# Taking the rest of a projection on VectorE, straight from the PSUM bank

## The reference

```python
x = x + LN(attention(LN(x)))
x = x + LN(experts(LN(x)))
```

```python
qkv = x @ W_in.T + b_in
scores = einsum("bhqd,bhkd->bhqk", q, k) * scale + mask
a = softmax(scores); o = a @ v; return o @ W_out.T + b_out
...
fused = w[0] * local_out + w[1] * global_out   # w = softmax(fusion_w)
```

## Time and profile before

| what | value |
|---|---|
| median of 3 runs | 1818.97 us (1818.25 to 1822.79) |
| the profiled execution | 1818.58 us, its span 1816.8 us |
| busy: PE, DVE | 1636.8 us, 1226.7 us |
| busy: ACT, POOL | 993.6 us, 884.3 us |

### The profile page before, as it was taken

How to read it: one execution, slowest core, us unless ns; L and a number is a source line. 1 busy time by engine, 2 the same in 40 slices (tenths; PEclk the granted TensorE clock), 3 DMA queues, 4 the chain that set the end, 5 groups by cost and what they waited for, 6 DMA issues and landing times.

```text
span 1816.8 us, 43072 instructions
## 1 busy us (share of the span) xinstructions
PE 1636.8 (90%) x14472; PEld 1184.8 (65%) x14472; DVE 1226.7 (68%) x3673; ACT 993.6 (55%) x2251; POOL 884.3 (49%) x1173
## 2 busy tenths in 40 slices
PE   5779999999999999999999999999999846999993
PEld 3457777777776676766676776777776634666662
DVE  2446777777777776777777777777777534777773
ACT  2356666666666666666666666666666531111210
POOL 3224545445445555545554444444444341666665
PEclk9789999999999999999999999999999967999997
DMA  6985555555555555555555555555555202444540
GB/s 138 222 181 98 95 96 97 96 95 96 97 94 96 96 96 94 95 94 94 93 92 91 91 93 94 94 92 94 92 84 97 67 13 74 146 138 140 153 126 10
DMA packets 254346, 183.59 MB, mean 101 GB/s; under 512 B 30116, under 2 KB 252775, under 8 KB 254142
## 3 DMA queue, kind: packets, MB, share of 16 engines
q1 hardware_dynamic: 245150, 176.22, 48.9%
q0 software_dynamic: 7168, 3.73, 1.2%
q10 hardware_dynamic: 1824, 1.06, 0.2%
HBM read 55.78 MB, written 38.04 MB: 52 GB/s over the span
## 4 chain that ended last, share of the span: by engine, by line
PE 59%; POOL 17%; issue 8%; DVE 6%; SPq 4%; ACT 3%; DVEq 2%; DMA 1%; POOLq 0%; ACTq 0%
PE bank L1147 11%; PE bank L1275 7%; PE bank L1184 5%; PE bank L1178 4%; PE bank L1129 4%; PE bank L1116 4%; PE bank L1137 3%; POOL out L632 3%; POOL zb L627 3%; PE bank L1175 3%; PE bank L1108 3%; PE bank L1104 3%; PE bank L1154 3%; SPq L422 2%; POOL ybuf L583 2%
## 5 line engine op out<-in xcount | busy, mean ns | idle before, releaser
L883 DVE TENSOR_REDUCE mx<-bank 128x2 f32<-128x512 f32 (+1 forms) x768 | 513.3, 685 | 134.1 <-PE bank L1175 87.2
L674 ACT ACTIVATE pt<-bank 128x512 f32<-128x512 f32 x768 | 448.2, 601 | 160.2 <-PE bank L1116 130.2
L550 POOL TENSOR_TENSOR rest<-x,parts 128x512 f32<-128x512 f32 x128 | 148.5, 1160 | 295.7 <-ACT x L688 295.7
L1147 PE MATMUL bank<-xnT,weff 128*128 128x256 f32 x1024 | 247.4, 385 | 2.4 <-ACT x L688 1.7
L1178 PE MATMUL bank<-stack 96*128 96x256 bf16 x1024 | 198.9, 276 | 20.6 <-DVE mx L883 19.6
L688 ACT ACTIVATE parts<-bank,bqk 128x256 bf16<-128x256 f32 x256 | 107.5, 471 | 173.4 <-PE bank L1147 160.4
L1147 PEld LDWEIGHTS bank<-xnT,weff 128*128 128x128 f32 x1024 | 185.9, 191 | 23.8 <-ACT x L688 2.1
L555 POOL TENSOR_TENSOR parts<-rest,parts 128x512 bf16<-128x512 f32 x128 | 148.4, 1160 | 107.7 <-DVE parts L871 107.7
L1116 PE MATMUL bank<-stack 100*128 100x128 bf16 x2048 | 198.9, 219 | 0.0
L1116 PEld LDWEIGHTS bank<-stack 100*128 100x128 bf16 x2048 | 158.9, 98 | 12.5
L1178 PEld LDWEIGHTS bank<-stack 96*128 96x128 bf16 x1024 | 79.5, 98 | 125.2 <-issue 57.4
(11 more groups left out here) (149 smaller groups left out, 3144.3 us busy)
## 6 DMA issues: line engine op xcount, KB each, us to landing
stack<-parts SPq DMA_DIRECT2D x384, 128.0 KB, 6.7
stack<-parts SPq DMA_DIRECT2D x768, 64.0 KB, 2.6
slots_scratch<-zeros SPq DMA_DIRECT2D x5, 2080.0 KB, 11.9
erows<-slots_scratch SPq DMA_DIRECT2D x64, 130.0 KB
xr<-x SPq DMA_DIRECT2D x32, 256.0 KB, 7.2
out<-obuf SPq DMA_DIRECT2D x32, 256.0 KB, 2.1
ew<-w_gate SPq DMA_DIRECT2D x32, 256.0 KB, 3.2
ew<-w_up SPq DMA_DIRECT2D x32, 256.0 KB, 3.5
```

The costliest lines, as they stand in the source:

```text
L550: pool.tensor_tensor(rest[:, j % 2, :], x32[:, j % 2, :], parts[:, j, 0, :], ALU.subtract).then_inc(rest_ready, 1)
L674: act.activation(pt[:, u % 8, :], S2[u % 2][:, :], ACT.Exp).then_inc(p_ready, 1)
L883: dve.reduce_max(dst, src, AX.X).then_inc(s1_read, 1)
L1147: last = pe.matmul(bank[:, t * WIN:(t + 1) * WIN], weff[:, b, c, qk * D + t * P:qk * D + (t + 1) * P], xnT[:, par, c, :], start=(c == 0), ...
```

## The change

ScalarE's full-width copy `x32` goes, and with it Pool's `remainder`. VectorE makes the rest itself, in two `scalar_tensor_tensor` instructions of 256 columns: bank plus bias minus high part. It then drains and casts as before. The scale of q (0.25), which ScalarE applied at each copy, is folded into the weights at the start, in two copies where one was. VectorE's piece j comes at one unit after p_j where it came at three. It waits for ScalarE's high part (`hi_ready`), and for Pool's low part of the piece before that used the same buffer of `rest`. The banks of `PJ` are now given back by `rest_ready`, VectorE's, and SyncE's first wait for a piece is for `hi_ready`.

```diff
-        x32 = sb("x32", [P, 2, 512])
...
-        PJ_USES = [("x2T", 4, x2T_ready, 1, 0), ("xnT", 0, xnT_ready, 1, 0), ("lg", 4, lg_ready, 1, 0), ("p0", 0, x32_ready, 4, 0),
+        PJ_USES = [("x2T", 4, x2T_ready, 1, 0), ("xnT", 0, xnT_ready, 1, 0), ("lg", 4, lg_ready, 1, 0), ("p0", 0, rest_ready, 4, 0),
...
-                for part, ready in enumerate((x32_ready, mid_ready, lo_ready)):
+                for part, ready in enumerate((hi_ready, mid_ready, lo_ready)):
...
-            def remainder(j, a):
-
-                wait(pool, x32_ready, a, 4, j)
-                if j < 2:
-                    wait(pool, mid_ready, back(a), 4, j + 2)
-                else:
-                    wait(pool, mid_ready, a, 4, j - 2)
-                pool.tensor_tensor(rest[:, j % 2, :], x32[:, j % 2, :], parts[:, j, 0, :], ALU.subtract
-                                   ).then_inc(rest_ready, 1)
...
-                    act.activation(weff[:, b, c, 0:512].rearrange("p (x d h) -> p x d h", d=HD, h=8),
-                                   banks[n][:, :].rearrange("p (x h d) -> p x d h", d=HD, h=8), ACT.Copy)
+                    for lo, scale in ((0, QSCALE), (256, 1.0)):
+                        act.activation(weff[:, b, c, lo:lo + 256].rearrange("p (x d h) -> p x d h", d=HD, h=8),
+                                       banks[n][:, lo:lo + 256].rearrange("p (x h d) -> p x d h", d=HD, h=8), ACT.Copy, scale=scale)
...
-            def projected_full(j, a):
-
-                wait(act, rest_ready, a if j >= 2 else back(a), 4, (j - 2) % 4)
-                projected(j, a, x32[:, j % 2, :]).then_inc(x32_ready, 1)
+                b, qk = j // 2, j % 2
+                for t in range(2):
+                    cols = slice(t * WIN, (t + 1) * WIN)
+                    last = act.activation(parts[:, j, 0, cols], pj_bank(f"p{j}")[:, cols], ACT.Identity,
+                                          bias=bqk[:, b, 2 * qk + t:2 * qk + t + 1])
+                last.then_inc(hi_ready, 1)
...
             def mid_part(j, a):
-                wait(dve, rest_ready, a, 4, j)
+                wait(dve, hi_ready, a, 4, j)
+                wait(dve, lo_ready, a if j >= 2 else back(a), 4, (j - 2) % 4)
+                b, qk = j // 2, j % 2
+                for t in range(2):
+                    cols = slice(t * WIN, (t + 1) * WIN)
+                    last = dve.scalar_tensor_tensor(rest[:, j % 2, cols], pj_bank(f"p{j}")[:, cols], bqk[:, b, 2 * qk + t:2 * qk + t + 1],
+                                                    parts[:, j, 0, cols], ALU.add, ALU.subtract)
+                last.then_inc(rest_ready, 1)
+                dve.drain()
                 dve.tensor_copy(parts[:, j, 1, :], rest[:, j % 2, :]).then_inc(mid_ready, 1)
...
-                        if a and k == AT[f"p{j}"] + 3:
+                        if a and k == AT[f"p{j}"] + 1:
                             mid_part(j, a)
```

More of the change, by code:

```diff
@@ L199, in attention_moe_program @@
         v_full = sem("v_full")
-        x32_ready = sem("x32_ready")
+        hi_ready = sem("hi_ready")
         rest_ready = sem("rest_ready")
@@ L265, in attention_moe_program @@
                    ("n_l0", 2, on_ready[0], 2, 0), ("n_l1", 2, on_ready[0], 2, 1), ("oT_l", 2, onT_ready[0], 1, 0)]
-        PJ_USES = [("x2T", 4, x2T_ready, 1, 0), ("xnT", 0, xnT_ready, 1, 0), ("lg", 4, lg_ready, 1, 0), ("p0", 0, x32_ready, 4, 0),
-                   ("p1", 0, x32_ready, 4, 1), ("cs", 4, cs_read, 1, 0), ("p2", 0, x32_ready, 4, 2), ("p3", 0, x32_ready, 4, 3),
+        PJ_USES = [("x2T", 4, x2T_ready, 1, 0), ("xnT", 0, xnT_ready, 1, 0), ("lg", 4, lg_ready, 1, 0), ("p0", 0, rest_ready, 4, 0),
+                   ("p1", 0, rest_ready, 4, 1), ("cs", 4, cs_read, 1, 0), ("p2", 0, rest_ready, 4, 2), ("p3", 0, rest_ready, 4, 3),
                    ("v0", 1, v_ready, 2, 0), ("v1", 1, v_ready, 2, 1)]
@@ L560, in step @@
                 nxt = back(s, -1)
-                if a:
-                    remainder(0, a)
                 if f:
@@ L567, in step @@
                     low_part(0, a)
-                    remainder(1, a)
                     low_part(1, a)
@@ L578, in step @@
                     inv_std(1, d)
-                if a:
-                    remainder(2, a)
                 if d:
@@ L589, in step @@
                     low_part(2, a)
-                    remainder(3, a)
                 if d:
@@ L681, in values_out @@
                 act.activation(OT[:, b, g % 4, :], PV[:, 0:WIN], ACT.Copy).then_inc(ot_ready, 1)
[L683 to L690, removed]
             def projected_high(j, a):
@@ L697, in projected_high @@
                         act.wait_ge(landed, nth(back(a), 96, 95))
-                projected(j, a, parts[:, j, 0, :])
-            def projected_full(j, a):
-                wait(act, rest_ready, a if j >= 2 else back(a), 4, (j - 2) % 4)
-                projected(j, a, x32[:, j % 2, :]).then_inc(x32_ready, 1)
+                b, qk = j // 2, j % 2
[4 more added lines that the diff above has]
+                last.then_inc(hi_ready, 1)
             def v_out(q, b, par):
@@ L759, in step @@
                             projected_high(j, a)
-                        if a and k == AT[f"p{j}"] + 1:
-                            projected_full(j, a)
                     if f and k == AT["gate"]:
```

## The result

The changed kernel takes 1769.4 us (median of 4 runs) against 1819.95 us before: ratio 0.972, 95% interval 0.9701 to 0.9739. Three of its four executions took 1769.17 to 1769.61 us; the fourth took 8928.17 us, is left out of the ratio, and nothing measured says why. Its profiled execution has a span of 1767.9 us against 1816.8. I had predicted 1781 us, with a range from 1753 to 1811, and faster with a chance of 0.83. The direction and the place were right; the gain came out at 49 us of the span and 50.5 of the median where I had worked out 38.

The account below looks back on a forecast made before the run. VectorE, queued behind Pool's chain, was taken to make TensorE stand in each step's second part. 1.95 - 0.29 - 0.36 = 1.30 us a step, times 29 is 37.7 us; 1818.6 - 37.7 gives 1781 us, range 1753 to 1811.

Parts of the forecast that it names:

- The bound: In a step's second part VectorE is late for TensorE, queued behind Pool's chain; TensorE stands 2.26 us a step.
- The costs on VectorE: Eight added instructions a step at 472 ns; a piece costs 0.95 us more with the drain, 3.8 us a step.
- The first part: Units 3 to 15: the added work fits, TensorE stays at 27.69 us, slack 0.7 us less 0.27 for the cast's wait.
- ScalarE at nothing, Pool's freed time at nothing: ScalarE's 3.8 us less work costed at nothing; of Pool's 4.6 us a step, one 1.13 us subtraction lies on the chain.
- VectorE's wait of 3.7 us in a step: VectorE's wait for Pool's `rest` at L550, 103.3 us in all, expected to go.
- The second part: From unit 15's maximum, starting 1.95 us earlier, to the splitting of the maxima: gain 1.30 us a step.
- two meetings with TensorE: VectorE meets TensorE's transposes for the second local half, losing 0.29 us, and the scores of unit 19, losing 0.36.
- The steps: Steps s = 3 to 31, 29 of them, taken as equal, gain 1.30 us each: 37.7 us.
- Full recovery: Rival: TensorE loses none of its time to VectorE; 65.5 us gained, 1753 us; chance 0.13.
- The cast's meeting with L570: Rival: piece 3's cast comes behind Pool's second `ybuf` instruction; only 0.4 us a step gained, 1807 us; chance 0.17.
- Slower: Rival: added VectorE instructions cost 881 ns each and hold TensorE in units 3 to 15; 1836 us; chance 0.09.
- the wait only moves: Rival: the second part ends when another thing does, such as the chain through `ybuf`; nothing gained, 1818 us; chance 0.08.

Follow-up runs that it names:

- e2b_clear: The kernel before with only Pool's order changed: rest of piece 3 right after the ybuf pair, low parts of pieces 2 and 3 later; 1784.63 us.
- e6_unit13: The changed kernel with one more VectorE instruction, a maximum over 352 constant columns, ahead of piece 3's pair; 1790.28 us.
- e2_swap: The kernel before with Pool making the rest of piece 3 ahead of the low part of piece 2; 1816.25 us.
- e1_late: The changed kernel with VectorE's piece put back to three units after its projection; 1782.47 us.
- e4_act: The changed kernel with two ScalarE instructions of 256 columns on constants one unit behind each projection; 1768.12 us.
- e3_pool: The changed kernel with four Pool subtractions of 512 columns on constants put in a step where the removed ones stood; 1773.21 us.
- e8_mT2: The changed kernel with the transposes of the split global maxima one unit later, at unit 2; 1749.51 us.
- e9_norm0: The changed kernel with VectorE's statistics of the next window moved to unit 8, their normalising to 18, Pool's inv_std(0) ahead of inv_std(1); 1765.58 us.

## Why the prediction was right, and where it was short

**The bound: right.** Shown by e2b_clear, which frees VectorE from one instruction of Pool's chain without removing an instruction and gives 35 us, and by the waits after.

**The costs on VectorE: right.** 477 ns where I took 472 from L1050, 0.87 us a pair as worked out, 0.09 us for the drain where I had 0.08. VectorE's busy time is 957.05 / 28 = 34.2 us in a step; I had said about 35. That the pair lets Pool run beside it, argued from L907, is shown by e6_unit13 and by the pair at 912.80.

**The first part: right.** It stayed at 27.70 us. The slack ahead of unit 15 is 0.51 us; I had 0.7 less the 0.27 for the cast's wait. The cast was 0.1 us longer and not 0.27. I had let it start when Pool's instruction is over and then take its whole 0.43 us. In each of the four traces shown here (the changed kernel, e2_swap, e1_late, e6_unit13) a cast that meets Pool ends 0.28 us behind the end of Pool's instruction, so the price is what is left of that instruction when the cast starts, less 0.15 us: 0.25 - 0.15 here.

**ScalarE at nothing, Pool's freed time at nothing: right and nearly right.** e4_act and e3_pool give -1.3 and +3.8 us, of 50.5.

**VectorE's wait of 3.7 us in a step** was read as one wait. It is two, 0.37 us ahead of piece 2's cast and 3.28 ahead of piece 3's (57 waits in 28 steps); only the second is the chain's. The sum does not use it.

**The second part: right in kind, mis-sized.** The maximum of unit 15 starts 0.42 us behind the start of its scores, as worked out (0.43). Then I subtracted two meetings with TensorE, 0.29 and 0.36 us, to come from 1.95 to 1.30 us a step. From the maximum of unit 15 the reciprocal of the second local half starts 3.44 us later; before it was 3.42, so the first meeting cost nothing. The maximum of unit 19 starts 5.99 us later, against 5.72: 0.27 us for both instead of 0.65. The step's gain is then 1.95 - 0.27 = 1.68, which is the difference of the median steps; the mean, 1.73, has 0.05 more from the unusual steps named above. (My two terms also held, unnamed, the 0.04 us that a maximum starts behind the end of its scores.) That VectorE has no idle time from unit 19 to the splitting holds for the usual step; the traced one had 0.43 us.

The reason is in how I placed TensorE without its stalls. I took them from the idle columns, 1.30 us up to those transposes. But from the scores of unit 15 to these transposes TensorE now takes 3.22 us; before it took 4.74, so it had stood 1.52. To the scores of unit 19 it takes 5.99 us now and took 7.68, a difference of 1.69. So there are 0.39 us in the stalls that the idle columns do not show, and the traces show where.

0.22 us is overlap. A gap in the idle column begins where the modelled end of the last product lies, and in an unstalled stretch the next product starts ahead of that end: the scores of unit 15 in the timeline above last until 915.96, while the instruction after them begins at 915.80. Of the other 0.17, 0.16 is in the transposes behind the second stall: from their start to the scores that follow it is 0.60 us before (949.35 to 949.95), and 0.44 now (918.80 to 919.24). TensorE's timeline before:

```profile
949.95 0.39 PE L1178 MATMUL bank<-stack 96*128 96x256 bf16 x2
```

The busy column agrees: for the same products TensorE counts as busy for 1161.23 / 28 = 41.47 us in a step before and 1150.62 / 28 = 41.09 after. Of the 1.73 us gained in a step, 1.35 come out of its idle time and 0.38 out of what counted as busy. All this is read from the two traces and was not tested by a run.

So the step that failed is the sum's last two terms, 0.29 and 0.36 us, which measured 0.02 and 0.25: TensorE came out of its stalls earlier than I placed it, and VectorE met it less. That is 0.38 us in a step, 11 of the 13 us by which the forecast was short.

**The steps: right.** 29 steps by 1.73 would be 50.2 us. 48.5 came in the 28 that were measured, and the 29th, a shorter one, gave 1.7 (38.38 to 36.69 us). The rest of the execution takes that 1.3 us longer. I had said that the steps are equal; they were so within 0.4 us.

**The rivals.** Full recovery did not come: TensorE still stands 0.87 us a step (25.1 in 29), where I had 0.96; e8_mT2 shows that it could. The cast's meeting with L570 did not happen, by 0.3 us, and e6_unit13 shows its price. Slower fell because the price of the pair was L1050's and not L941's. That the wait only moves fell with VectorE's idle 0.51 us ahead of unit 15 and no wait at `ybuf`.

**The rule on ports.** The prediction weighed what the Trainium skill says in "SBUF — State Buffer", Who interferes with whom. e2_swap, e1_late and e6_unit13 agree with it: a cast from SBUF to SBUF that arrives 0.08 to 0.22 us behind the start of a long Pool instruction takes 1.33 to 1.47 us instead of 0.43, and the pair with one operand in the bank does not stretch. Its other direction, Pool waiting for the cast, is there too, and small: L570 takes 1.33 us in the traced step where it took 1.27, and not the 0.35 us more that I had given it. It starts 0.21 us ahead of the cast's end and pays 0.06; in e6_unit13 Pool's L545 starts 0.33 us ahead of it and takes 1.34 us instead of 1.16. Both are again the remainder less 0.15 us.

What stays open: why the first `ybuf` lies 2.1 us later than before. It lies between 154.36 and 157.24 us in the traces of the variants of the changed kernel, so it may be no effect of the change; I made no run for it. Open as well is what VectorE stands for in the unusual steps.

## What to carry to other kernels

When one engine is late for the bound engine, ask which queue its late instruction stands in, not how busy anyone is. Here VectorE waited for the last of four Pool instructions, and reordering Pool gave two thirds of what the whole change gave. Before a VectorE cast or copy within SBUF is moved, look at what Pool runs at that moment: 0.4 us of work in the wrong place cost 0.7 us a step, and the reordering alone gave 4 or 35 us according to which Pool instruction came next. A cast that meets Pool pays what is left of Pool's instruction, less 0.15 us here. And to place TensorE without its stalls, measure from start to start in a stretch without stalls; the idle columns leave some of each stall out. Compare the median step too: a single traced step can be an unusual one.

## What the runs showed of the hardware that was not expected

A short Pool instruction does not hold up VectorE as a long one does. In the changed kernel VectorE normalises `xn` from 882.20 us, two instructions in 0.73 us, as everywhere in this kernel, while Pool's power of two columns runs from 882.06 for 0.69 us. VectorE's and Pool's timelines:

```profile
882.20 0.73 DVE L803 TENSOR_SCALAR xn<-xw,mv,rstd 128x256 f32<-128x256 f32 x2
...
882.06 0.69 POOL L535 TENSOR_TENSOR rstd<-ve,mhalf 128x2 f32<-128x2 f32 x1
```

In e9_norm0 the same two instructions come 0.35 us behind the start of Pool's residual sum over 512 columns, and take 1.39 us:

```profile
917.16 1.39 DVE L803 TENSOR_SCALAR xn<-xw,mv,rstd 128x256 f32<-128x256 f32 x2
...
916.81 1.27 POOL L587 TENSOR_TENSOR xrow<-ybuf,xr 128x512 f32<-128x512 f32 x1
```

So the VectorE instructions are not ones that never wait for Pool. Which part of the short one holds nothing up is not shown.
